# Reordering the first chunks of a test-time-training scan inside a fused decoder block

## The chip, the cores and the metric

One Trainium2 chip, one of its cores. The metric is device time in microseconds (us) for one execution of the whole program.

## The reference, cut to what matters

The program is one decoder block: a test-time-training (TTT) linear attention, a cross-attention and a quantised gated FFN, each followed by a residual sum and a layer norm. The input is 16 sequences of 64 tokens with 256 features. The change touches only the first part, a scan over four chunks of 16 tokens that carries a 16x16 state S for every sequence and head:

```python
def step(S, inp):
    qi, ki, vi, ei = inp
    kh = jnp.einsum('bchd,bhde->bche', ki, S)
    target = vi - ki
    mu = jnp.mean(kh, -1, keepdims=True)
    rstd = jax.lax.rsqrt(jnp.var(kh, -1, keepdims=True) + EPS)
    kh_hat = (kh - mu) * rstd
    g = w * kh_hat + b - target
    gw = g * w
    v_new = (gw - jnp.mean(gw, -1, keepdims=True) - kh_hat * jnp.mean(gw * kh_hat, -1, keepdims=True)) * rstd
    A = jnp.einsum('bchd,bshd->bhcs', qi, ki)
    A = jnp.where(tri, A, 0.0) * jnp.transpose(ei, (0, 2, 1))[:, :, None, :]
    qh = jnp.einsum('bchd,bhde->bche', qi, S) - jnp.einsum('bhcs,bshe->bche', A, v_new)
    o = qi + _ln(qh, w, b)
    S = S - jnp.einsum('bchd,bche->bhde', ki * ei[..., None], v_new)
    return (S, o)
S_fin, o = jax.lax.scan(step, S0, (qc, kc, vc, ec))
```

S starts at zero. Afterwards `o` is gated, normalised per head and multiplied with `Wo`; the cross-attention's keys (`ctx @ Wk`, 16 heads of 128) are independent of the scan.

## The kernel before, in words

Every engine runs a hand-written program in its own order; semaphores tie them together, and there is no planner. The scan's 16 heads lie in two halves of eight, h = 0 and 1, and its four chunks are c = 0 to 3. For a chunk and half the engines do this:

- TensorE (PE): `state_products(c, h)` multiplies the chunk's keys and queries with the state (L538); `scores_ttt(c, h)` makes the scores A (L520 for chunks 0 and 1, L514 for 2 and 3); `own_terms(c, h)` multiplies the corrections with A and the keys, which gives qh and the new state (L548). All are trains of small tiles: 128 recorded matmuls and 128 weight loads a time (64 and 64 for L514).
- VectorE (DVE): `state_read` (L1483 to L1486) takes the products from PSUM; `chain` (L1498 to L1518) turns them into corrections `ub`; `after_own_terms` (L1569, L1573) takes qh and the new state out of PSUM; `a_masked` (L1470) masks the scores and `kb_rows` (L1465) transposes the keys for the own terms; `out_normed`, `out_gated`, `out_c` finish the outputs. Two wide preparations stand ahead of chunk 1: `output_terms` (eight products, L1557, and a transpose, L1560) and `gate_terms` (L1565), which waits for ScalarE's two scalings of the gate (L1097).
- ScalarE (ACT) takes the square roots between `state_read` and `chain` (L1117), squares outputs, spreads keys (`k_blocks`, `k_quads`) and takes the cross-attention keys out of PSUM (L1105, L1107).

Between these steps PE makes the cross-attention keys in 32 units (`key_unit`: two recorded matmuls, L682; after every fourth unit eight short ones, L672, sum the squares of four). `KEY_PLACES` says how many units stand at each place; PE and ACT read the same list. Unit n writes bank 6 or 7 and waits until ACT has emptied unit n - 2.

PE's order ahead of the scan is: a list of jobs (weight transposes and products, the last being `s2` and `w2t`), with `scores_ttt(0, ...)`, `scores_ttt(1, ...)` and `own_terms(0, 0)` put in between; then all jobs must be emptied before the first key unit, and `own_terms(0, 1)` follows that unit.

SyncE (SP) issues the loads in order. Two stand in the scan:

```python
            sp.wait_ge(sem("mg_done"), 2 * 2)
            load_xwq(0)
            load_x()
            roots_to_rows(0)
            sp.wait_ge(sem("og_ready"), 2)
            load_xwq(1)
            load_xwq(2)
            scales_out(0)
            sp.wait_ge(sem("mg_done"), 2 * NCH)
```

`mg_done` counts the own terms (4 is `own_terms(1, 1)`), `og_ready` the gated outputs (2 is `out_gated(1)`). `scales_out(0)` waits for `key_scales(0)` on DVE (L1616), and `load_xwq(3)`, the key scales `rkb` and `ctx` stand behind it.

Of the kernel before, what the change touches and what calls it, by code (L numbers as in the profile page):

```python
# [31 lines left out]
ALU = mybir.AluOpType  # L32
# [6 lines left out]
NCH = T // C  # L39
KT = D // P  # L40
# [12 lines left out]
GW = 2 * C + 32  # L53
NKU = 2 * XH
LT = NT - 1
KEY_PLACES = [(1, 2), (2, 2, 1, 1, 2, 1), (2, 2, 1, 1, 2, 1), (2, 3, 4, 2)]

def decoder_block(nc, x, ctx_in, Wq, Wk, Wv, Wo, Wbeta, ln_w, ln_b, Wg1, Wg2, norm_w,  # L60
                  XWq, XWk, XWv, XWo, gq, gk, w1_in, w2_in, out):
    stack = ExitStack()
    with stack:
# [164 lines left out]
        def bank(n, w=BANK, at=0):  # L228
            return ps[:, n * BANK + at:n * BANK + at + w]
# [6 lines left out]
        def sem(name):  # L236
            if name not in sems:
                sems[name] = stack.enter_context(nc.semaphore(name))
            return sems[name]
# [78 lines left out]
            job("w2t", n, by="act")  # L318
        index_of = {(k, key): n for n, (k, key, _) in enumerate(jobs)}
        job_banks = [n % 8 for n in range(index_of[("s1", (0,))])]  # L320
        job_banks += [(5, 6, 7, 0, 1, 2, 3)[n % 7] for n in range(len(jobs) - 1 - len(job_banks))] + [5]

        def bank_left(n):
            return max(m for m in range(n) if job_banks[m] == job_banks[n])
# [155 lines left out]
        def _(pe):  # L480
# [11 lines left out]
            def done(ins):  # L492
                ins.then_inc(sem("job_done"), 1)
# [7 lines left out]
            def scores_ttt(c, h):  # L501
                if h == 0:
                    if c < 2:
                        pe.wait_ge(sem("kb_ready"), 2 * (c + 1))
                    else:
                        pe.wait_ge(sem("kbq_ready"), 4 * (c - 1))
                    if c >= 1:
                        pe.wait_ge(sem("at_ready"), c)
                if c >= 2:
                    for g in range(B):  # L510
                        for part in (slice(0, 64), slice(64, P)):
                            col = ((c * G + h * B + g) * 2 + 1) * C
                            out = 4 * BANK + (h * B + g) * C
                            last = mm(ps[part, out:out + C], kbq_f[part, h, g * 64:(g + 1) * 64],  # L514
                                      kq[part, col:col + C], start=True, stop=True)
                    last.then_inc(sem("a_done"), 1)
                    return
                for g, j, part in tiles(h):
                    col = ((c * G + g) * 2 + 1) * C
                    last = mm(ps[part, 4 * BANK + g * C:4 * BANK + (g + 1) * C], kb[part, g * 32:(g + 1) * 32],  # L520
                              kq[part, col:col + C], start=True, stop=True)
                last.then_inc(sem("a_done"), 1)
# [19 lines left out]
            def own_terms(c, h):  # L542
                pe.wait_ge(sem("at_ready"), c + 1)
                pe.wait_ge(sem("kbr_ready"), c + 1)
                pe.wait_ge(sem("ub_ready"), 4 * (2 * c + h + 1))
                w = C + 32 if c < NCH - 1 else C
                for g, j, part in tiles(h):
                    last = mm(ps[part, g * GW + C:g * GW + C + w], ub[part, g * 32:(g + 1) * 32],  # L548
                              ak[part, g * (C + 32):g * (C + 32) + w],
                              start=c == 0 and g % (BANK // GW) == 0, stop=True, skip_group_check=True)  # L550
                last.then_inc(sem("mg_done"), 1)
# [81 lines left out]
            for n in range(8):  # L633
# [4 lines left out]
                done(last)  # L638
                if n == 3:
                    scores_ttt(1, 0)  # L640
            scores_ttt(1, 1)
            wait(emptied_by(index_of[("s1", (2,))]))
            pe.wait_ge(sem("diag_ready"), 2)
            bk = open_job("s2", 0)
# [4 lines left out]
            for n in range(2):  # L649
                bk = open_job("w2t", n)  # L650
                o = bank(bk).bitcast(BF16)
                for t in range(3):
                    k = n * 3 + t
                    w = P if k < NK2 - 1 else FFL
                    for r in range(KT):
                        last = nc.tensor.transpose(o[0:w, (t * KT + r) * P:(t * KT + r + 1) * P],
                                                   w2q[:, r * FF + k * P:r * FF + k * P + w], ident_b[:, :])
                done(last)


            def warm(bk, n):
# [33 lines left out]
                    key_unit(next(units))  # L695

            keys(KEY_PLACES[0][0])
            own_terms(0, 1)
            keys(KEY_PLACES[0][1])
            for c in range(1, NCH):  # L700
                places = iter(KEY_PLACES[c])
                state_products(c, 0)
                keys(next(places))
                state_products(c, 1)
                keys(next(places))
                if c < NCH - 1:
                    scores_ttt(c + 1, 0)
                    keys(next(places))
                own_terms(c, 0)
                if c < NCH - 1:  # L710
                    keys(next(places))
                    scores_ttt(c + 1, 1)
                keys(next(places))
                own_terms(c, 1)
                for n in places:
                    keys(n)
# [259 lines left out]
        def _(act):  # L976
# [9 lines left out]
            def emptied(ins):  # L986
                ins.then_inc(sem("prep_act"), 1)

            def job_at(kind, *key):
                n = index_of[(kind, key)]  # L990
                act.wait_ge(sem("job_done"), n + 1)
                return job_banks[n]
# [91 lines left out]
                emptied(A(mvo[:, n * BANK:(n + 1) * BANK], bank(bk), ACT.Copy))  # L1084
            bk = job_at("s2", 0)
            emptied(A(s2[:, :], bank(bk, D), ACT.Copy))
            bk = job_at("w2t", 0)
            emptied(A(w2t[:, 0:3 * D], bank(bk).bitcast(BF16)[:, 0:3 * D], ACT.Copy))
            bk = job_at("w2t", 1)
# [51 lines left out]
            def output_root(n):  # L1141
                root_of(ovs[:, :], osd[:, :], "ovs_ready", n, "osd_ready")
# [8 lines left out]
            def keys(n):  # L1151
                for _ in range(n):
                    key_unit(next(units))

            keys(KEY_PLACES[0][0])
            A(eps_t[:, 2:3], eps_t[:, 1:2], ACT.Sqrt)
            keys(KEY_PLACES[0][1])
            for c in range(1, NCH):
                places = KEY_PLACES[c]
                state_root(c, 0)  # L1160
                if c >= 2:
                    output_root(2 * c - 2)
                output_square(c - 1)
                keys(places[0])
                if c < NCH - 1:
                    k_quads(c + 1)
                keys(places[1])
                output_root(2 * c - 1)
                state_root(c, 1)
                if c < NCH - 1:  # L1170
                    k_blocks(c + 1)
                for n in places[2:-2]:
                    keys(n)
                keys(places[-2])
                if c < NCH - 1:
                    gated_square(c - 1)
                    keys(places[-1])
# [182 lines left out]
        def _(dve):  # L1360
# [172 lines left out]
            def first_chains():  # L1533
# [16 lines left out]
                for h in range(2):  # L1550
                    u_blocks(0, h)

            def output_terms():
                dve.wait_ge(sem("prep_act"), emptied_by(index_of[("gate", (1, 1))])[1])
                for hh in range(KT):
                    for c in range(NCH):
                        V.scalar_tensor_tensor(out=chunk_half(sgR, c, hh), in0=kq_half(1, c, hh), scalar=wb[:, KT + hh:KT + hh + 1],  # L1557
                                               in1=chunk_half(tmp1, c, hh), op0=ALU.add, op1=ALU.mult).then_inc(sem("q_terms"), 1)
                dve.wait_ge(sem("q_terms"), KT * NCH)
                V.transpose(qbR[:, :], sgR[:, :]).then_inc(sem("out_terms"), 1)  # L1560

# [59 lines left out]
            first_chains()  # L1621
            for c in range(1, NCH):
                p_rows(c)
            output_terms()
            after_own_terms(0, 0)
            gate_terms()
            after_own_terms(0, 1)
            for c in range(1, NCH):
                if c == 1:
                    kb_rows(c)  # L1630
                    a_masked(c)
                if c == NCH - 1:
                    key_scales(0)
                state_read(c, 0)
                if c >= 2:
                    kb_rows(c)
                    a_masked(c)
                    output_inverse(2 * c - 2)
                    out_c(c - 2)
                chain(c, 0)  # L1640
                state_read(c, 1)
                output_sums(2 * c - 1)
                output_inverse(2 * c - 1)
                chain(c, 1)
                out_normed()
                after_own_terms(c, 0)
                if c < NCH - 1:
                    out_gated(c - 1)
                else:
                    gated_part(0)  # L1650
                after_own_terms(c, 1)
                if c < NCH - 1:
                    output_sums(2 * c)
# [49 lines left out]
            last_out(0)  # L1703
            last_square(qhR, 2)
            gated_part(1)


            def turn(kind, i, n=0):
# [331 lines left out]
```

## Time and profile before

| | |
|---|---|
| time, median of 3 runs | 373.15 us (372.58 to 373.59) |
| the profiled execution | 372.6 us |
| its span, first to last instruction | 370.9 us |
| mean granted TensorE clock | 0.995 of full speed |
| PE busy | 338.8 us (91%) |
| DVE busy | 265.1 us (71%) |
| ACT busy | 206.9 us (56%) |

The scan runs from about 58 to 141 us of the span; what comes after it is the cross-attention and the FFN. The trace gives for each instruction its engine, its line in the kernel and what released it. "issue" is time in which an engine waited for nothing that the profile shows. The DMA queue called "instruction" carries the engines' own programs.

### The profile page before, as it was taken

The numbers are of one execution on the slowest core, as the hardware profiler recorded it, in microseconds if no ns is written. First come the engines' busy times: TensorE is split into PE (matmuls) and PEld (weight loads), VectorE is DVE, ScalarE is ACT, GpSimd is POOL, SyncE is SP. The second block draws the span as 40 slices with busy tenths as digits, with TensorE's granted clock in tenths as the row PEclk, the third lists the DMA queues.
The fourth block names the chain that finished last, engine by engine and source line by source line (L and its number), as shares of the span: only waits on it lengthen the run. The fifth ranks groups of instructions, "written<-read, shape, count | busy, mean of one in ns | idle before, by whom it ended". The sixth has DMA issues, their size and how long they took to land.

```text
span 370.9 us, 11150 instructions
## 1 busy us (share of the span) xinstructions
PE 338.8 (91%) x4833; PEld 242.4 (65%) x4836; DVE 265.1 (71%) x544; ACT 206.9 (56%) x382; POOL 75.5 (20%) x91
## 2 busy tenths in 40 slices
PE   0999997999899789898999999999999999999974
PEld 0644685565555334787796896987977969866732
DVE  0499989799799999856442855946748549476795
ACT  1245984895665474537246555565565547575351
POOL 3009300000000000000340521623515306300100
PEclk9999999999999899999999999999999999999999
DMA  8998000000502205800050200201101000000000
GB/s 184 281 271 298 4 4 4 4 4 6 171 4 55 75 3 140 151 5 0 4 117 2 58 0 16 60 0 44 30 16 57 2 17 2 0 16 1 16 1 28
DMA packets 17985, 19.94 MB, mean 54 GB/s; under 512 B 3712, under 2 KB 15376, under 8 KB 17680
## 3 DMA queue, kind: packets, MB, share of 16 engines
q1 hardware_dynamic: 17328, 18.69, 19.1%
q10 hardware_dynamic: 608, 0.54, 0.7%
q8 instruction: 38, 0.62, 0.7%
q14 instruction: 11, 0.09, 0.1%
HBM read 18.04 MB, written 1.18 MB: 52 GB/s over the span
## 4 chain that ended last, share of the span: by engine, by line
PE 68%; DVE 22%; ACT 4%; issue 2%; DMA 2%; SPq 0%; POOL 0%; POOLq 0%; DVEq 0%
PE ps L812 14%; PE ps L746 13%; PE ps L567 6%; PE ps L804 5%; PE ps L789 4%; PE ps L831 3%; PE ps L762 2%; PE ps L637 2%; PE ps L682 2%; PE ps L780 2%; DMA xn<-in_x_dram 2%; PE ps L858 1%; PE ps L520 1%; PE ps L548 1%; PE ps L849 1%
## 5 line engine op out<-in xcount | busy, mean ns | idle before, releaser
L746 PEld LDWEIGHTS ps<-x1t,xwq 128*128 128x128 f32 x512 | 59.2, 192 | 6.0 <-issue 4.2
L746 PE MATMUL ps<-x1t,xwq 128*128 128x128 f32 x512 | 62.1, 278 | 0.5 <-ACT x1t L1238 0.5
L812 PE MATMUL ps<-mvo,cxp 128*128 128x256 f32 x224 | 51.8, 383 | 0.5 <-ACT cxp L1249 0.5
L1982 POOL TENSOR_SCALAR rstd<-mv 128x1 f32<-128x1 f32 x20 | 4.4, 218 | 203.2 <-DVE mv L1721 203.2
L812 PEld LDWEIGHTS ps<-mvo,cxp 128*128 128x128 f32 x224 | 41.3, 190 | 6.6 <-ACT cxp L1249 0.8
L1201 ACT ACTIVATE qt<-ps 128x512 f32<-128x512 f32 x32 | 19.1, 596 | 31.7 <-PE ps L746 31.7
L682 PE MATMUL ps<-ctxt,xwk 128*128 128x512 f32 x64 | 34.5, 648 | 1.6 <-ACT w2t L1091 1.2
L1105 ACT ACTIVATE ksq<-ps 128x512 f32<-128x512 f32 x32 | 18.9, 591 | 12.5 <-PE ps L682 8.4
L1107 ACT ACTIVATE kt<-ps,gks 128x512 f32<-128x512 f32 x32 | 22.0, 686 | 0.0
L1208 ACT ACTIVATE qsq<-ps 128x512 f32<-128x512 f32 x32 | 19.0, 593 | 3.2 <-PE ps L762 3.1
L789 PEld LDWEIGHTS ps<-kt,qt 128*64 128x64 f32 x512 | 16.2, 138 | 6.8 <-ACT qt L1201 3.8
L1730 DVE TENSOR_SCALAR x<-rr,mv,rstd 128x256 f32<-128x256 f32 x16 | 6.6, 412 | 18.7 <-POOL rstd L1983 18.5
L804 PE MATMUL ps<-pt,ctx 64*128 64x512 f32 x64 | 18.2, 638 | 0.7 <-ACT pt L1228 0.7
L789 PE MATMUL ps<-kt,qt 128*64 128x64 f32 x512 | 18.4, 225 | 0.0
L682 PEld LDWEIGHTS ps<-ctxt,xwk 128*128 128x128 f32 x64 | 10.8, 197 | 11.4 <-issue 6.5
L1769 DVE TENSOR_TENSOR gs<-ps,s 128x352 f32<-128x352 f32 x16 | 8.3, 523 | 13.4 <-PE ps L831 13.2
L1249 ACT ACTIVATE cxp<-ps 128x512 f32<-128x512 f32 x28 | 15.3, 605 | 4.5 <-PE ps L804 4.5
L1997 POOL TENSOR_TENSOR rq<-rq,mhalf 128x16 f32<-128x16 f32 x6 | 17.4, 2908 | 0.5
L548 PEld LDWEIGHTS ps<-ak,ub 32*32 32x32 f32 x1024 | 11.0, 105 | 9.2 <-issue 9.2
L538 PEld LDWEIGHTS ps<-kqi,st 32*32 32x32 f32 x768 | 10.4, 108 | 9.5 <-issue 9.5
L1793 DVE TENSOR_TENSOR pr<-ps,rkb 128x1024 f32<-128x1024 f32 x8 | 9.8, 1225 | 8.7 <-PE ps L789 8.7
L538 PE MATMUL ps<-kqi,st 32*32 32x64 f32 (+1 forms) x768 | 11.7, 212 | 4.4 <-issue 4.4
(252 smaller groups left out, 692.8 us busy)
## 6 DMA issues: line engine op xcount, KB each, us to landing
rkb<-kscale SPq DMA_DIRECT2D x16, 256.0 KB, 4.3
ctx<-in_ctx_dram SPq DMA_DIRECT2D x4, 512.0 KB, 7.7
xwo<-in_L_xattn_Wo_dram SPq DMA_DIRECT2D x1, 2048.0 KB, 14.2
xwq<-in_L_xattn_Wq_dram SPq DMA_DIRECT2D x4, 512.0 KB, 4.3
w1n<-in_L_ffn_w_gate_up_dram SPq DMA_DIRECT2D x1, 1408.0 KB, 10.1
xwv<-in_L_xattn_Wv_dram SPq DMA_DIRECT2D x1, 1024.0 KB, 11.9
xwk<-in_L_xattn_Wk_dram SPq DMA_DIRECT2D x1, 1024.0 KB, 16.4
xn<-in_x_dram SPq DMA_DIRECT2D x2, 512.0 KB, 6.6
```

What stands on the lines that cost most here:

```text
L538: last = mm(out, st[part, g * 32:(g + 1) * 32], moving, start=g % (BANK // GW) == 0, stop=False, skip_group_check=True)
L567: last = mm(bank(bk), w[:, k * D + hh * P:k * D + (hh + 1) * P], xt[:, k * B * T + half * BANK:k * B * T + (half + 1) * BANK], start=k == ...
L682: mm(bank(6 + n % 2), xwk[:, h * XD:(h + 1) * XD], ctxt[:, half * BANK:(half + 1) * BANK], start=True, stop=True)\
L746: last = mm(bank(n % 2, P, t * P), xwq[qn][:, k * BANK + t * P:k * BANK + (t + 1) * P], x1t[:, (i % 2) * D + k * P:(i % 2) * D + (k + 1) * ...
L789: last = mm(ps[b2 * T:(b2 + 1) * T, 4 * BANK + h * T:4 * BANK + (h + 1) * T], qt[:, h * P + b2 * T:h * P + (b2 + 1) * T], kt[:, (i * XH + ...
L804: turn_done(mm(bank(bk), ctx2[rows, b * CD:(b + 1) * CD], pt[rows, :].rearrange("p (h q) -> p h q", q=P)[:, :, b2 * T:(b2 + 1) * T], start ...
L812: last = mm(bank(turn_banks[turn_of[("y", i, 0)]], D), context_of(i)[:, h * P:(h + 1) * P], mvo[:, h * D:(h + 1) * D], start=h == 0, stop= ...
L1105: A(ksq[n % 4][:, :], bank(6 + n % 2), ACT.Square).then_inc(sem("k_squared"), 1)
L1107: A(o, bank(6 + n % 2).rearrange("p (i t) -> p i t", t=P), ACT.Copy, scale=gks[:, 1:2]).then_inc(sem("key_emptied"), 1)
L1201: A(qt[:, qn * BANK:(qn + 1) * BANK], bank(n % 2), ACT.Copy).then_inc(sem("q_copied"), 1)
L1208: A(qsq[:, (n % 2) * BANK:(n % 2 + 1) * BANK], bank(n % 2), ACT.Square).then_inc(sem("q_squared"), 1)
L1997: GP.tensor_tensor(rq[:, :], rq[:, :], mhalf[:, :], ALU.pow).then_inc(sem("rq_ready"), 1)
```

## The change

On PE, `own_terms(0, 1)` and `state_products(1, 0)` move up behind `own_terms(0, 0)` and the job `w2t`, ahead of all key units; `scores_ttt(1, 1)` moves back behind two key units; and in chunk 1 `own_terms(1, 0)` goes ahead of `scores_ttt(2, 0)`. Chunk 1 holds fewer key units (5 for 9), chunk 2 one more (10) and chunk 3 three more (14). Job `w2t` 0 uses bank 6 instead of 7. On DVE, `output_terms` is split: its eight products are interleaved with `after_own_terms(0, ...)` and its transpose stands behind `kb_rows(1)`; `gate_terms` moves behind `after_own_terms(1, 0)`, `a_masked(1)` behind `chain(1, 0)`, and `key_scales(0)` from the start of chunk 3 to the end of the scan. ACT's program follows.

```diff
 GW = 2 * C + 32
 NKU = 2 * XH
 LT = NT - 1
-KEY_PLACES = [(1, 2), (2, 2, 1, 1, 2, 1), (2, 2, 1, 1, 2, 1), (2, 3, 4, 2)]
+KEY_PLACES = [(2, 1), (1, 3, 1), (2, 2, 2, 1, 2, 1), (3, 4, 5, 2)]
 
 
 
             job("w2t", n, by="act")
         index_of = {(k, key): n for n, (k, key, _) in enumerate(jobs)}
         job_banks = [n % 8 for n in range(index_of[("s1", (0,))])]
-        job_banks += [(5, 6, 7, 0, 1, 2, 3)[n % 7] for n in range(len(jobs) - 1 - len(job_banks))] + [5]
+        job_banks += [(5, 6, 7, 0, 1, 2, 3)[n % 7] for n in range(len(jobs) - 2 - len(job_banks))] + [6, 5]
 
         def bank_left(n):
             return max(m for m in range(n) if job_banks[m] == job_banks[n])
                 done(last)
                 if n == 3:
                     scores_ttt(1, 0)
-            scores_ttt(1, 1)
             wait(emptied_by(index_of[("s1", (2,))]))
             pe.wait_ge(sem("diag_ready"), 2)
             bk = open_job("s2", 0)
                         last = nc.tensor.transpose(o[0:w, (t * KT + r) * P:(t * KT + r + 1) * P],
                                                    w2q[:, r * FF + k * P:r * FF + k * P + w], ident_b[:, :])
                 done(last)
+            wait(emptied_by(index_of[("s2", (0,))]))
+            own_terms(0, 1)
+            state_products(1, 0)
 
 
             def warm(bk, n):
                     key_unit(next(units))
 
             keys(KEY_PLACES[0][0])
-            own_terms(0, 1)
+            scores_ttt(1, 1)
             keys(KEY_PLACES[0][1])
-            for c in range(1, NCH):
+            state_products(1, 1)
+            keys(KEY_PLACES[1][0])
+            own_terms(1, 0)
+            scores_ttt(2, 0)
+            keys(KEY_PLACES[1][1])
+            own_terms(1, 1)
+            scores_ttt(2, 1)
+            keys(KEY_PLACES[1][2])
+            for c in range(2, NCH):
                 places = iter(KEY_PLACES[c])
                 state_products(c, 0)
                 keys(next(places))
                 emptied(A(mvo[:, n * BANK:(n + 1) * BANK], bank(bk), ACT.Copy))
             bk = job_at("s2", 0)
             emptied(A(s2[:, :], bank(bk, D), ACT.Copy))
+            A(eps_t[:, 2:3], eps_t[:, 1:2], ACT.Sqrt)
             bk = job_at("w2t", 0)
             emptied(A(w2t[:, 0:3 * D], bank(bk).bitcast(BF16)[:, 0:3 * D], ACT.Copy))
             bk = job_at("w2t", 1)
                 for _ in range(n):
                     key_unit(next(units))
 
-            keys(KEY_PLACES[0][0])
-            A(eps_t[:, 2:3], eps_t[:, 1:2], ACT.Sqrt)
-            keys(KEY_PLACES[0][1])
-            for c in range(1, NCH):
+            state_root(1, 0)
+            output_square(0)
+            keys(sum(KEY_PLACES[0]))
+            k_quads(2)
+            output_root(1)
+            state_root(1, 1)
+            k_blocks(2)
+            keys(KEY_PLACES[1][0] + KEY_PLACES[1][1])
+            gated_square(0)
+            keys(KEY_PLACES[1][2])
+            for c in range(2, NCH):
                 places = KEY_PLACES[c]
                 state_root(c, 0)
-                if c >= 2:
-                    output_root(2 * c - 2)
+                output_root(2 * c - 2)
                 output_square(c - 1)
                 keys(places[0])
                 if c < NCH - 1:
                 for h in range(2):
                     u_blocks(0, h)
 
+            def query_terms(hh):
+                dve.wait_ge(sem("prep_act"), emptied_by(index_of[("gate", (1, 1))])[1])
+                for c in range(NCH):
+                    V.scalar_tensor_tensor(out=chunk_half(sgR, c, hh), in0=kq_half(1, c, hh), scalar=wb[:, KT + hh:KT + hh + 1],
+                                           in1=chunk_half(tmp1, c, hh), op0=ALU.add, op1=ALU.mult).then_inc(sem("q_terms"), 1)
+
             def output_terms():
-                dve.wait_ge(sem("prep_act"), emptied_by(index_of[("gate", (1, 1))])[1])
-                for hh in range(KT):
-                    for c in range(NCH):
-                        V.scalar_tensor_tensor(out=chunk_half(sgR, c, hh), in0=kq_half(1, c, hh), scalar=wb[:, KT + hh:KT + hh + 1],
-                                               in1=chunk_half(tmp1, c, hh), op0=ALU.add, op1=ALU.mult).then_inc(sem("q_terms"), 1)
                 dve.wait_ge(sem("q_terms"), KT * NCH)
                 V.transpose(qbR[:, :], sgR[:, :]).then_inc(sem("out_terms"), 1)
 
             first_chains()
             for c in range(1, NCH):
                 p_rows(c)
+            query_terms(0)
+            after_own_terms(0, 0)
+            query_terms(1)
+            after_own_terms(0, 1)
+            kb_rows(1)
             output_terms()
-            after_own_terms(0, 0)
-            gate_terms()
-            after_own_terms(0, 1)
             for c in range(1, NCH):
-                if c == 1:
-                    kb_rows(c)
-                    a_masked(c)
-                if c == NCH - 1:
-                    key_scales(0)
                 state_read(c, 0)
                 if c >= 2:
                     kb_rows(c)
                     output_inverse(2 * c - 2)
                     out_c(c - 2)
                 chain(c, 0)
+                if c == 1:
+                    a_masked(c)
                 state_read(c, 1)
                 output_sums(2 * c - 1)
                 output_inverse(2 * c - 1)
                 chain(c, 1)
                 out_normed()
                 after_own_terms(c, 0)
+                if c == 1:
+                    gate_terms()
                 if c < NCH - 1:
                     out_gated(c - 1)
                 else:
             last_out(0)
             last_square(qhR, 2)
             gated_part(1)
+            key_scales(0)
 
 
             def turn(kind, i, n=0):
```

## Rows read from the trace of the kernel before

**Rows 1.** The page: the chain that ended last by engine, and the instruction queue.
```profile
q8 instruction: 38, 0.62, 0.7%
...
PE 68%; DVE 22%; ACT 4%; issue 2%; DMA 2%; SPq 0%; POOL 0%; POOLq 0%; DVEq 0%
```

**Rows 2.** Timeline of DVE, 57 to 120 us: start, us, line, operation, count.
```profile
57.98 3.21 DVE L1557 SCALAR_TENSOR_TENSOR sgR<-kqi,wb,tmp 128x256 f32<-128x256 f32 x8
61.23 2.31 DVE L1560 STREAM_TRANSPOSE qbR<-sgR 128x2048 f32<-128x2048 f32 x1
...
66.99 2.31 DVE L1565 STREAM_TRANSPOSE sgR<-tmp 128x2048 f32<-128x2048 f32 x1 [2.37 <-ACT tmp L1097]
...
70.31 1.20 DVE L1465 STREAM_TRANSPOSE ak<-kb 128x1024 f32<-128x1024 f32 x1
...
72.01 0.43 DVE L1483 STREAM_TRANSPOSE khR<-ps 128x256 f32<-128x256 f32 x1
...
73.73 0.25 DVE L1498 RECIPROCAL rs<-sdc 128x16 f32<-128x16 f32 x1 [0.38 <-ACT sdc L1117]
...
82.35 0.25 DVE L1498 RECIPROCAL rs<-sdc 128x16 f32<-128x16 f32 x1
...
88.23 0.69 DVE L1589 TENSOR_TENSOR oR<-qhR,ors 128x512 f32<-128x512 f32 x1
...
91.72 0.45 DVE L1569 STREAM_TRANSPOSE qhR<-ps 128x256 f32<-128x256 f32 x1 [0.27 <-PE ps L548]
...
92.84 0.65 DVE L1577 TENSOR_REDUCE ovs<-osq 128x32 f32<-128x512 f32 x1
95.30 0.45 DVE L1483 STREAM_TRANSPOSE khR<-ps 128x256 f32<-128x256 f32 x1 [1.81 <-PE ps L538]
...
117.75 0.45 DVE L1569 STREAM_TRANSPOSE qhR<-ps 128x256 f32<-128x256 f32 x1
...
119.44 0.54 DVE L1616 RECIPROCAL kinv<-kinv 128x64 f32<-128x64 f32 x1
119.90 0.39 DVE L1483 STREAM_TRANSPOSE khR<-ps 128x256 f32<-128x256 f32 x1
```

**Rows 3.** Timeline of PE, 57 to 130 us: start, us, line, operation, count, wait.
```profile
61.72 1.13 PE L548 MATMUL ps<-ak,ub 32*32 32x48 f32 x87 [1.52 <-issue]
...
85.14 1.07 PE L672 MATMUL ps<-ksq,onehot 128*32 128x512 f32 x8
86.13 2.04 PE L514 MATMUL ps<-kqi,kbq 64*64 64x16 f32 x64
88.10 1.98 PE L682 MATMUL ps<-ctxt,xwk 128*128 128x512 f32 x4
90.02 1.56 PE L548 MATMUL ps<-ak,ub 32*32 32x48 f32 x128
...
94.82 0.42 PE L538 MATMUL ps<-kqi,st 32*32 32x64 f32 x15 [0.45 <-issue]
...
124.83 1.07 PE L538 MATMUL ps<-kqi,st 32*32 32x32 f32 x64 [2.60 <-issue]
125.84 3.17 PE L682 MATMUL ps<-ctxt,xwk 128*128 128x512 f32 x4
```

**Rows 4.** Busy time and instruction counts of each engine in stretches; then PEclk, DMA.
```profile
61.70:94.50 32.80, 31.00 (x1020) 19.56 (x1021) 27.30 (x58) 23.94 (x42) 0.00 (x0) 1.00 0.06 19
...
122.30:128.30 6.00, 3.46 (x67) 2.12 (x68) 5.69 (x14) 2.44 (x5) 0.00 (x0) 0.72 0.07 19
```

**Rows 5.** DMA queues in three windows: 92.0 to 92.5, 92.5 to 98.8, 98.8 to 101.0 us.
```profile
q8 instruction: 1, 0.02, 14.3%
...
q1 hardware_dynamic: 1250, 1.50, 77.6%
...
q8 instruction: 1, 0.02, 2.9%
```

**Rows 6.** Timeline of SP's queue, 80 to 125 us: issue start, us, transfer.
```profile
91.64 0.38 SPq L388 DMA_DIRECT2D xwq<-in_L_xattn_Wq_dram  x1
```

## The prediction

> **What bounds the kernel now.** I read the chain that ended last first. Over the whole run it is mostly PE [rows 1], but in the scan it changes hands: PE up to 95.30 us, where DVE waits for PE's product [rows 2], and DVE from there to the scan's end. So I then read DVE's timeline [rows 2], where the reader should look at start times, since one start less the one before it is what a step costs in its queue, and at the bracket, the idle time ahead of it. DVE is nearly always at work; its two large gaps ahead of chunk 2 are 2.37 us ahead of `gate_terms` and 1.81 us ahead of `state_read(2, 0)` at 95.30, where it waits for PE. From 95.30 on its order is the same in both kernels, so a delay or gain of that read goes to the end, unless PE falls behind.
>
> PE's timeline [rows 3] shows why it may. Its small-tile trains stop four times between 57 and 130 us with the remark "issue": 1.52, 0.45, 1.37 and 2.60 us (three of the four stand there). The instruction counts between the first two stops are 1020 + 1021 = 2041 [rows 4], eight times 256 but for seven, and the view does not count separate waits; the queue "instruction" moved 0.62 MB in 38 packets, 16 KB each [rows 1]. So I take PE to get its program in blocks of 256, and a stop to be a block that came late. The block of the 0.45 us stop was fetched just after 92.0 us and could be used at 94.82; the next one was not fetched until after 98.8 [rows 5], though its turn came at 94.82 when PE went on. In between, 1.50 MB of SP's first load (issued at 91.64 [rows 6]) passed. The 2.60 us stop is the same thing after SP's second load, which `out_gated(1)` releases at 117.75 [rows 2]. Fetches asked for during a load waited for about its tail; I saw three of three do so.
>
> **The change part by part: DVE.** I lay its new order end to end. The products of half 0, 57.98 to 59.6 (four of eight in 3.21 us). `own_terms(0, 0)` now starts without the `scores_ttt(1, 1)` that stood ahead of it, near 58.4, and takes 1.5 (as 90.02 to 91.51, rounded from [rows 3]): 59.9. Taking it out costs 1.1 (91.72 to 92.84): 61.1. Products of half 1: 62.7. `own_terms(0, 1)` follows `w2t` (0.9) but crosses a block's edge so soon after the last one that I give it a stop of 1.3, near the 1.52 [rows 3] that `own_terms(0, 0)` loses: it ends at 63.6 and DVE waits 0.9. Out: 64.8; `kb_rows` 1.1 and the wide transpose 2.25: 68.2. `state_read(1, 0)` starts here, not at 72.01, and PE's product for it is done by 67.4 (63.6, 1.9 of work and one more stop, up to 1.9). Read and root 1.7 (72.01 to 73.73); from one chain's start to the next 8.6 (73.73 to 82.35) plus `a_masked` 0.6; chain 5.9; out_normed, out of PSUM and gating 3.2 (88.23 to 91.72 less 0.27); `gate_terms` 2.3, whose scalings are long done; out again 1.1, sums 0.6. That ends at 92.2, 3.1 before 95.30 [rows 2]. ACT's earlier square-root table (its load lies beside PE's transposes) costs nothing here: `w2t` is not needed until the key units near 67.4. If that cover were gone, it would delay key units only.
>
> **PE in the same stretch** keeps up: `own_terms(1, 1)` ends at 87.1 (four units and the stops put PE 0.5 behind DVE's corrections at 85.0), then scores 2.0, a unit 1.0 and `state_products(2, 0)` 1.9: 92.0. So far the change is worth 3 us.
>
> **The load.** `own_terms(1, 1)` at 87.1 releases SP's first load, 4.5 us earlier than before, since the wait is on that step. Its traffic runs to about 94.4 (as 91.64 to 98.9 [rows 5, 6]). In the kernel before, a block ends 226 instructions into `state_products(2, 0)`'s 256 (all but 15 of 128 matmuls with their loads [rows 3]). The change takes four key units and four sums, 32 instructions, out of what precedes it and adds one wait, so the edge comes 257 after its start: in the key unit right behind it. That block can be asked for when the one before is begun, 256 earlier, at 89 to 90. Before, that moment lay ahead of the load's first byte (fetched at 92.0, load from 92.5); now it lies inside it. Fetched at 94.4 and usable 2.3 later (before it was 2.3 to 2.8, from 92.0 to 92.5 until 94.82), it lets PE go on at 96.7, after a stop of 4.6 us. A 2.60 us stop was followed by the lower granted clock (1.2 GHz level; mean 0.72 over 122.3 to 128.3 [rows 4]), under which four key matmuls took 3.17, not 1.98 [rows 3]; I charge up to 1.6 for it here, that 1.2 and some 0.4 for the rest of the stretch.
>
> What is late next: from 96.7 PE has 20.4 us of work to the end of `own_terms(2, 1)` (half a unit 0.5, eight units 8.0, three sets of sums 3.0, two scores 4.0, a product 1.9, two own terms 3.0 [rows 3]): 117.1, or 118.7 with the clock. DVE wants it 22.4 after its read (95.30 to 117.75), at 114.7. ACT empties these late units ahead of `output_root(3)`, for which DVE's chain waits about 1 more. So DVE waits 2 to 3 us, and its `out_gated(1)` releases SP's second load near 116, just ahead of the fetch that `state_products(3, 0)` needs (asked for near 118). That fetch comes at the load's tail, 120.5 (4.7 after its release: before, 117.75, and usable at 124.83, so fetched near 122.5), and is usable at 122.8; before, the same load hit the next block, which DVE did not need yet. `state_products(3, 0)` ends at 123.4 to 124, so `state_read(3, 0)` is at 123.5 to 124.1, not 119.90: 3.6 to 4.2 late.
>
> **The rest.** `key_scales(0)` leaves a place where PE is now the later one and adds 0.46 (119.44 to 119.90) where DVE sets the end. Chunk 3's three extra units (1.25 us each with their sums) fill PE's idle time but leave `own_terms(3, 0)` and `(3, 1)` just at DVE's heels: 0.4. SP's queue behind `scales_out(0)`, with `load_xwq(3)`, `rkb` and `ctx`, starts only after the scan's tail; the first of them is wanted by PE's fourth query quarter, after the first norms, so I charge nothing and leave up to 1 us to the range; a miss would show as PE waiting at L746. Sum: 3.9 + 0.5 + 0.4 = 4.8 us over the profiled 372.6, 377.4. The median shown stands 0.55 above that execution; I forecast 377.6.
>
> **Weighed against the skill.** The trace shows four stops at block edges [rows 3]. The Trainium skill, "Runtime: NRT & Kernel Launch", section "Instruction fetch mechanics", says that the sequencer fetches 256-instruction blocks by itself and that the cost is mostly hidden. The block's size agrees with [rows 1]; the hiding does not hold in these trains, and by it the time would be that of rival 2. For the fetch's place in a load, "DMA: Bandwidth & Descriptors" of the Trainium skill, section "Queues, rings and completion order", has an engine take turns between rings packet by packet; [rows 5] shows a wait to the tail, and by the page the time would be that of rival 1.
>
> **Rivals.** *1. The loads do not hold blocks back.* Then PE stops only 1.1 after `state_products(2, 0)` (asked for at 90, 0.8 to start, 2.3 to use) and ends `own_terms(2, 1)` about 114 to 115, even with DVE's 114.7; chunk 3 loses 1 to another edge and 0.9 as above. DVE's 3.1 is used up: 0 ± 0.7, 373.2. For it: one block went by just ahead of the load. Against: three fetches that waited. *2. No block is ever late, or edges fall harmlessly.* DVE reads at 91.3, `state_products(3, 0)` ends at 116.7, 3.2 early, less 0.5, 0.4 and about 0.6 of new waits on key units: 1.7 faster, 371.4. This one ends on the other side; it decides if the stop behind `state_products(2, 0)` stays under about 1 us. *3. Only one load hits*: 2.3 to 4.0 slower, 376. *4. The edge lies a few instructions earlier*, inside `state_products(2, 0)`: DVE itself waits until 97, and the second load follows: 9 to 10 slower, 383.
>
> **How the numbers follow.** Changes under 0.3% (1.1 us) are about what a measurement of this kernel cannot tell from none. Forecast 0.46 (its own range 375.5 to 379.8, from a fetch at two thirds of the load without the clock's price to the full one with it); rival 1 0.18, rival 2 0.20, rival 3 0.11, rival 4 0.05. Slower 0.46 + 0.11 + 0.05 = 0.62, same 0.18, faster 0.20. The range 371.9 to 380 leaves out rival 4 and most of rival 2.
>
> **What would show it.** Right: `state_read(2, 0)` near 92 instead of 95.30; then a stop of 4 to 5 us marked "issue" at a key unit (L682) behind L538 near 92, a lower granted clock after it, DVE waiting ahead of L1569 or L1483 near 115 to 124, SP's first load near 87. Wrong: no such stop, or a stop that DVE never waits for; then the 3 us stay. If `state_read(2, 0)` itself is not early, my sum over DVE's queue failed.

## The result, and the profile after

The changed kernel takes 378.89 us (median of 4, 378.18 to 379.12) against 373.37 for the kernel before in the same comparison: slower, ratio 1.0134, 95% interval 1.0092 to 1.0176. The profiled execution took 379.12 us with a span of 377.4 and a mean granted clock of 0.982 (before: 372.6, 370.9, 0.995). The forecast was 377.6. Ratios here and below leave out runs more than 1.5% above the fastest of their kernel; medians are over all runs.

The whole difference is in the scan: the first `rw` behind it (DVE's first residual sum) starts at 154.10 instead of 147.45, 6.65 us later, and the spans of the two profiled executions differ by 6.5. Where it went is plainest in the view of waits, for DVE from 57 to 148 us: operation, what it waited for, us in total, times, the longest. First the kernel before, then the kernel after.

```profile
DVE sgR L1565 <- ACT tmp L1097: 2.4, 1, 2.4
DVE khR L1483 <- PE ps L538: 1.8, 1, 1.8
DVE ors L1581 <- ACT osd L1117: 1.2, 3, 0.4
DVE rs L1498 <- ACT sdc L1117: 0.4, 1, 0.4
DVE qhR L1569 <- PE ps L548: 0.3, 1, 0.3
```

```profile
DVE khR L1500 <- PE ps L538: 5.1, 3, 3.1
DVE qhR L1587 <- PE ps L548: 3.8, 4, 2.9
DVE ors L1599 <- ACT osd L1128: 3.4, 3, 1.7
DVE rs L1515 <- ACT sdc L1128: 0.4, 1, 0.4
```

The wait ahead of `gate_terms` (`sgR`) is gone, as meant. In its place DVE waits 3.3 us more for state products, 3.5 more for own terms and 2.2 more for roots: 12.7 us, not 6.1. These waits are 6.6 of the 6.65 us. PE's timeline after shows why it is late (start, us, line, tiles, count, idle before); these lines answer to [rows 3].

```profile
65.06 1.64 PE L538 MATMUL ps<-kqi,st 32*32 32x64 f32 x101 [1.91 <-issue]
66.63 1.98 PE L684 MATMUL ps<-ctxt,xwk 128*128 128x512 f32 x4
...
77.46 0.69 PE L514 MATMUL ps<-kqi,kbq 64*64 64x16 f32 x17
79.46 2.18 PE L514 MATMUL ps<-kqi,kbq 64*64 64x16 f32 x47 [1.30 <-issue]
81.57 2.07 PE L684 MATMUL ps<-ctxt,xwk 128*128 128x512 f32 x2
83.58 1.94 PE L674 MATMUL ps<-ksq,onehot 128*32 128x512 f32 x8
85.44 2.74 PE L684 MATMUL ps<-ctxt,xwk 128*128 128x512 f32 x4
88.11 1.56 PE L548 MATMUL ps<-ak,ub 32*32 32x48 f32 x128
...
92.63 1.99 PE L538 MATMUL ps<-kqi,st 32*32 32x64 f32 x128
94.55 0.70 PE L684 MATMUL ps<-ctxt,xwk 128*128 128x512 f32 x1
98.18 1.22 PE L684 MATMUL ps<-ctxt,xwk 128*128 128x512 f32 x1 [2.93 <-issue]
99.33 1.94 PE L674 MATMUL ps<-ksq,onehot 128*32 128x512 f32 x8
...
119.95 1.56 PE L548 MATMUL ps<-ak,ub 32*32 32x48 f32 x128
...
124.43 0.59 PE L538 MATMUL ps<-kqi,st 32*32 32x32 f32 x45 [1.03 <-issue]
```

Two stops matter: 1.30 us inside `scores_ttt(2, 0)` and 2.93 in the key unit behind `state_products(2, 0)`. Behind each, eight key sums take 1.94 us where they took 1.07 [rows 3]. The windows of these stretches give the reason. Each line has the stretch, its length, the busy time of PE, PE's weight loads, DVE, ACT and POOL, then the granted clock and the DMA share. The clock is 0.57 and 0.50 of full speed, the 1.2 GHz level for most or all of the stretch.

```profile
79.45:87.40 7.95, 7.94 (x60) 3.73 (x60) 7.63 (x18) 1.98 (x5) 0.00 (x0) 0.57 0.01 2
98.20:103.20 5.00, 5.00 (x11) 0.97 (x11) 4.72 (x11) 1.18 (x2) 0.00 (x0) 0.50 0.02 3
```

The second stop has SP's load in it, as [rows 5] had it for another block. The DMA queues after, in 89.6 to 95.7 us (the load alone, no packet of the instruction queue) and in 95.7 to 98.2 (the load's last 0.09 MB and the block):

```profile
q1 hardware_dynamic: 1224, 1.48, 77.0%
...
q8 instruction: 1, 0.02, 2.8%
```

DVE's timeline after, to be held against [rows 2]:

```profile
90.94 0.64 DVE L1595 TENSOR_REDUCE ovs<-osq 128x32 f32<-128x512 f32 x1
94.69 0.45 DVE L1500 STREAM_TRANSPOSE khR<-ps 128x256 f32<-128x256 f32 x1 [3.11 <-PE ps L538]
...
121.65 0.45 DVE L1587 STREAM_TRANSPOSE qhR<-ps 128x256 f32<-128x256 f32 x1 [2.85 <-PE ps L548]
...
125.07 0.45 DVE L1500 STREAM_TRANSPOSE khR<-ps 128x256 f32<-128x256 f32 x1 [1.65 <-PE ps L538]
...
138.95 0.35 DVE L1599 RECIPROCAL ors<-osd 128x32 f32<-128x32 f32 x1 [1.36 <-ACT osd L1128]
...
153.63 0.55 DVE L1634 RECIPROCAL kinv<-kinv 128x64 f32<-128x64 f32 x1
154.10 0.36 DVE L1864 TENSOR_TENSOR rw<-ps,xn 128x256 f32<-128x256 f32 x1
```

### The profile page after: what moved, and what is told of

Same layout as the page of the kernel before. It is cut to its first block, busy times and chain, and to the rows that moved or that the text cites. A ratio compares the mean times of both kernels' runs of the same rounds, so it can differ in the third digit from the quotient of the medians.

```text
span 377.4 us, 11154 instructions
## 1 busy us (share of the span) xinstructions
PE 343.3 (91%) x4836; PEld 243.4 (65%) x4836; DVE 265.3 (70%) x544; ACT 207.3 (55%) x382; POOL 75.6 (20%) x91
## 4 chain that ended last, share of the span: by engine, by line
PE 75%; DVE 15%; ACT 4%; issue 3%; DMA 2%; SPq 0%; POOL 0%; POOLq 0%; DVEq 0%; ACTq 0%
PE ps L822 14%; PE ps L756 13%; PE ps L684 6%; PE ps L567 5%; PE ps L814 5%; PE ps L799 4%; PE ps L548 3%; PE ps L841 3%; PE ps L514 2%; PE ps L772 2%; PE ps L674 2%; PE ps L637 2%; PE ps L538 2%; PE ps L790 2%; DMA xn<-in_x_dram 2%
## 5 line engine op out<-in xcount | busy, mean ns | idle before, releaser
L684 PE MATMUL ps<-ctxt,xwk 128*128 128x512 f32 x64 | 37.2, 685 | 6.0 <-ACT kt L1118 3.1
```

Of the source, the lines that this page charges most:

```text
L684: mm(bank(6 + n % 2), xwk[:, h * XD:(h + 1) * XD], ctxt[:, half * BANK:(half + 1) * BANK], start=True, stop=True)\
```

## The experiments

Theory 1: program blocks that come late, SP's load on top of them and the lower clock behind them make PE late. (An edge is the place in PE's program where one block of 256 instructions ends and the next begins.) Theory 2: the key units were handed out badly, with ACT emptying them in order. Theory 3: DVE's moved steps cost by themselves. The list of waits speaks against theory 3 already, since nearly all of the loss is time in which DVE waits for PE or ACT.

**The load, 12 us later.** In the kernel after and, as a control, in the kernel before:

```diff
 sp.wait_ge(sem("mg_done"), 2 * 2)
+sp.wait_ge(sem("kh_done"), 4)
 load_xwq(0)
 load_x()
```

> The kernel after, with SP's first load (the query weights and x, 1.5 MB) released by the second state product of chunk 2 instead of by own_terms(1, 1): some 12 us later, and behind the program block that stopped PE for 2.93 us in key unit 8. Theory 1 (program blocks that come late, one of them held back by this load, make PE late, and the lower clock after a stop adds to it): the stop at key unit 8 falls from 2.93 to 0.5 to 1.1 us, the key units behind it run at full clock, DVE's wait of 2.85 ahead of the copy for own_terms(2, 1) goes to under 1, state_read(3, 0) is at 121.5 to 122.5 instead of 125.07, and the total is 2.5 to 3.5 us less than the kernel after, 375.4 to 376.4. Theory 2 (the key units were handed out badly, and ACT, which empties them in order, is late with the roots): the order on PE and ACT is untouched, so less than 1 us. Theory 3 (the steps moved on DVE cost by themselves): less than 0.5 us.

> Control: the same later release of SP's first load in the kernel before. There the block held back by that load comes due while DVE has PE's results in hand, so theory 1 expects a smaller stop on PE in chunk 2 and 0 to 0.5 us off the total (372.9 to 373.4). Were the load costly in some other way (traffic of its own beside DVE and ACT), the total would fall by 1 us or more here too. Theories 2 and 3: no change.

After: 375.88 us, ratio to before 1.0085 (1.0055 to 1.0114). PE's timeline: the stop in the key unit is 0.91, the sums behind it take 1.07.

```profile
96.20 0.70 PE L685 MATMUL ps<-ctxt,xwk 128*128 128x512 f32 x1 [0.91 <-issue]
96.82 1.07 PE L675 MATMUL ps<-ksq,onehot 128*32 128x512 f32 x8
```

`state_read(3, 0)` starts at 121.30 (0.2 sooner than forecast), and DVE's wait ahead of the copy for `own_terms(2, 1)` is 0.64, as theory 1 said. The same edit in the kernel before gives 374.21, ratio 1.003 (0.9998 to 1.0061), above the 372.9 to 373.4 that I expected: in its trace the stops of 0.45 and 1.37 are gone (one of 0.21 is left), and still there is no gain. So the load costs through the block it holds back, where DVE waits for that block's work, and not by its traffic.

**The edges alone.** Only the places where PE's program is cut are moved, by matmuls at the start where PE idles until 8.2 us: 64 of them, half a block, and 128, a whole block, as the control.

```diff
 pe.wait_ge(sem("consts"), 2)
+for _ in range(64):
+    mm(bank(7)[0:32, 0:32], ident_b[0:32, 0:32], ident_b[0:32, 0:32], start=True, stop=True)
```

> The kernel after, with 64 matmuls of 32 columns (128 instructions) put ahead of PE's first work, where PE otherwise idles until 8.2 us: nothing in the scan's order changes, only the places at which PE's program is cut into blocks of 256 move by half a block. Theory 1: the stops marked issue appear at other instructions, and the total moves by 1 us or more; I expect 2 us less than the kernel after, 377, with half the chance that an edge lands inside a state product and it is 1 us more. Theories 2 and 3: within 0.5 us of the kernel after.

> Control for the run with half a block: 128 such matmuls (256 instructions), one whole block, so that the edges fall on the same instructions of the scan again while PE does twice the extra work at the start. Theory 1: the stops at the same instructions as in the kernel after and the total within 0.5 us of it. If the extra work at the start matters by itself (warmer clock, other fetches at the start), this run moves as the one with half a block does.

A whole block: 378.93 us (1.0154, 1.0109 to 1.0198), the kernel after again, with its stop in the same key unit (3.38). Half a block: 384.27 (1.0287, 1.0232 to 1.0341), 5.3 us slower than that, though every order is the same; its fastest run, 380.75, lies above the slowest with a whole block, 380.02. Theories 2 and 3 have no place for it. I had the sign wrong. PE's timeline of the half block shows the stops elsewhere:

```profile
82.23 1.06 PE L676 MATMUL ps<-ksq,onehot 128*32 128x512 f32 x8
...
85.66 1.56 PE L548 MATMUL ps<-ak,ub 32*32 32x48 f32 x128
...
89.03 1.93 PE L514 MATMUL ps<-kqi,kbq 64*64 64x16 f32 x61 [1.60 <-issue]
...
95.78 1.09 PE L538 MATMUL ps<-kqi,st 32*32 32x64 f32 x63 [1.08 <-issue]
```

Without a stop in `scores_ttt(2, 0)` the sums take 1.06 and `own_terms(1, 1)` starts at 85.66 instead of 88.11. But the next block, due inside `state_products(2, 0)` itself, was fetched only near the load's tail (load issued at 87.28, fetch at 93.39, use at 95.78), and DVE waits 4.53 for that product. This is rival 4's mechanism.

**The edge of the change, in the kernel before.** 112 such matmuls put the edge behind `state_products(2, 0)`, as after; then the same with the later load.

> The kernel before, with 112 matmuls of 32 columns (224 instructions) ahead of PE's first work, in time in which PE idles. All orders are those of before; the program edge that fell 226 instructions after the start of state_products(2, 0) now falls 258 after it, in the key unit behind, which is where the change puts it (257). Theory 1 (an edge there asks for its block inside SP's first load and stops PE in the key unit): a stop of 3 to 5 us marked issue at the key unit behind state_products(2, 0), where before had 0.45 inside the product, DVE waiting for PE late in chunk 2, and a total 3 to 5 us above before, 376.5 to 378 on the scale of 373.4. Theory 2 (the handing out of the key units) and theory 3 (the steps moved on DVE): neither is touched, so within 0.5 us of before.

> The kernel before with its edges moved by 224 instructions, as in the run before_edge_moved, whose times fell into two groups (370.8 to 376.3 and 377.6 to 379.8), and with the first load released 12 us later. Theory 1 (the two groups are a race of one block's fetch against the first byte of the load): the upper group is gone, all times between 371 and 375, median 372 to 373.5. If something else makes the two groups: they are there again.

376.94 us over 12 runs, but in two groups: 370.83 to 376.26 and 377.62 to 379.80. The ratio of 1.0024 (0.9986 to 1.0063) is of the lower group. The profiled run, 374.17, is of that group: its fetch, at 92.91, went through in the middle of the load (issued at 90.15, traffic until 97.9), and the stop was 1.25. So a load does not hold back every fetch. With the later load the median is 374.67 (0.9986, 0.9948 to 1.0024), again in two groups (371.29 to 373.20 and 376.14 to 379.99), so the race that I expected between load and fetch is not what makes the two groups. They go with the granted clock: over both kernels it is 0.991 to 0.993 in ten of the twelve lower runs and 0.974 to 0.986 in eleven of the twelve upper ones. The two traces, 374.17 and (with the later load) 376.91, show one place of it: in both PE waits 3.03 us for DVE in chunk 3, and behind that wait the clock is at the lower level for about twice as long in the second (a mean of 0.81 and of 0.62; fields as above).

```profile
132.00:141.00 9.00, 7.87 (x159) 3.31 (x163) 8.16 (x24) 4.86 (x10) 0.00 (x0) 0.81 0.01 3
133.00:142.00 9.00, 8.63 (x143) 3.88 (x144) 8.16 (x25) 3.24 (x7) 0.00 (x0) 0.62 0.01 3
```

Why the same wait is followed by more or less of it stays open. The edge there alone did not make the kernel slower in every run; this prediction of theory 1 held for half of them and not for the cause given.

**DVE's part alone.** The kernel before with `gate_terms` moved as in the change:

```diff
 after_own_terms(0, 0)
-gate_terms()
 after_own_terms(0, 1)
...
     after_own_terms(c, 0)
+    if c == 1:
+        gate_terms()
```

> One part of the change alone: the kernel before, with DVE's gate_terms moved from chunk 0 behind the first own terms of chunk 1, as the change has it; PE, ACT and SP keep the orders of before, so every block edge stays. If DVE sets chunk 1's time, its wait of 2.37 goes and the total falls by 1 to 2 us. If PE does (the trace has state_products(1, 0) at 69.40 only because own_terms(0, 1) and key units stand ahead of it): state_read(1, 0) moves by 0.5 at most, the wait ahead of state_read(2, 0) shrinks from 1.81 toward 0, and the total stays within 0.5 us of before.

373.04 us, ratio 1.0000 (0.9975 to 1.0024). The wait of 2.37 is replaced by one of 3.06 ahead of the copy for `own_terms(0, 1)`, and `state_read(1, 0)` is at 71.81 instead of 72.01. The move is worth nothing unless PE is sooner, and costs nothing either. Of DVE's moved steps only this one was tested alone; for the others theory 3 falls by the list of waits.

**Is PE in hand behind chunk 1?** First, ACT takes chunk 3's roots two key units sooner:

```diff
-keys(places[1])
+late = 2 if c == NCH - 1 else 0
+keys(places[1] - late)
 output_root(2 * c - 1)
 state_root(c, 1)
+keys(late)
```

> The kernel after, with ACT taking the two roots of chunk 3 (output_root(5), state_root(3, 1)) behind the fifth of chunk 3's key units instead of the seventh; PE, DVE and SP untouched. Theory 2: DVE's wait of 1.36 us ahead of output_inverse(5) falls to about 0.4 and the total by 0.5 to 1.0 us (377.9 to 378.4). Theory 1 alone: PE sets the end there, ACT's place does not matter, within 0.3 us of the kernel after.

DVE's wait fell from 1.36 to 0.39 as theory 2 said, and the total rose to 382.44 (1.0269, 1.0238 to 1.0301). PE's key sums now wait for ACT, and the own terms behind them come late. In the traces this makes the scan 2.0 us longer; another 1.2 us lies behind the scan (below). PE's timeline, then DVE's:

```profile
138.80 1.05 PE L674 MATMUL ps<-ksq,onehot 128*32 128x512 f32 x2 [1.24 <-ACT ksq L1116]
```

```profile
148.84 0.45 DVE L1589 STREAM_TRANSPOSE qhR<-ps 128x256 f32<-128x256 f32 x1 [2.80 <-PE ps L548]
```

Second, with the later load, what DVE waits for in chunk 2 is put sooner on PE:

```diff
 own_terms(1, 1)
+state_products(2, 0)
 scores_ttt(2, 1)
...
 for c in range(2, NCH):
...
-    state_products(c, 0)
+    if c > 2:
+        state_products(c, 0)
```

> The kernel with the later first load (375.9), and state_products(2, 0) ahead of scores_ttt(2, 1) on PE, so that DVE gets what it waits 3.0 us for some 2 us sooner. It asks whether what DVE loses there is lost for good or whether PE is the late engine through all of chunk 2 anyway. As the prediction had it (DVE sets the end from state_read(2, 0) on): state_read(2, 0) at 92.6 to 93.2 instead of 94.73, and the total 1.5 to 2 us less, 374. If PE's own work sets the end of chunk 2 (its work is only put in another order): state_read(2, 0) as early, but DVE waits as much more ahead of the copy for own_terms(2, 1) or of state_read(3, 0), and the total within 0.5 us of 375.9.

`state_read(2, 0)` came at 92.64, 2.1 sooner, and the total was 378.73 (1.0153, 1.0114 to 1.0193), 2.9 more than 375.88. Both forecasts miss: PE stopped 1.43 inside the product and went on at a clock of 0.58 (92.5 to 100.6), and ACT, in order, held `output_root(2)` behind a key unit that was now late. One run of the six had a granted clock of 0.991 and took 374.73, near the first forecast; the other five had 0.973 to 0.986 and took 377.76 to 379.42. So the miss is one of the clock at least in part. DVE's timeline:

```profile
92.64 0.45 DVE L1503 STREAM_TRANSPOSE khR<-ps 128x256 f32<-128x256 f32 x1 [1.64 <-PE ps L539]
...
98.91 0.35 DVE L1602 RECIPROCAL ors<-osd 128x32 f32<-128x32 f32 x1 [2.92 <-ACT osd L1131]
```

**The first stop.** The later load, and 80 matmuls at the start, which put the edge of `scores_ttt(2, 0)` behind it:

> The kernel with the later first load (375.9), and 80 matmuls of 32 columns (160 instructions) ahead of PE's first work, which moves the program edge that lay inside scores_ttt(2, 0) (a stop of 1.30 us in the kernel after, 1.57 with the later load) behind it, among key units; orders unchanged. Theory 1 (that stop and the lower clock behind it cost PE 2.5 us, and PE is the late engine from there to the end): no stop in scores_ttt(2, 0), the eight key sums behind it in about 1.06 us instead of 1.94, own_terms(1, 1) at 85.5 to 86 instead of 88.15, and the total 1.5 to 2.5 us less than 375.9, 373.4 to 374.4. If the clock's fall there is not from the stop, the sums take 1.9 again. If DVE's slack ahead of gate_terms hides it, the total stays within 0.5 us of 375.9.

The step itself went as expected: at 81.41 the eight sums take 1.06, the clock is 1.00 from 79.4 to 87.4, and `own_terms(1, 1)` starts at 85.59. The total did not: 383.71 (1.0283, 1.0253 to 1.0313), since all later edges moved too. PE's timeline:

```profile
85.59 1.43 PE L549 MATMUL ps<-ak,ub 32*32 32x48 f32 x115 [0.69 <-DVE ub L1538]
89.25 0.36 PE L549 MATMUL ps<-ak,ub 32*32 32x48 f32 x13 [2.23 <-issue]
...
131.53 0.31 PE L539 MATMUL ps<-kqi,st 32*32 32x32 f32 x12 [3.32 <-issue]
131.78 5.66 PE L687 MATMUL ps<-ctxt,xwk 128*128 128x512 f32 x8
```

The 3.32 us is SP's second load: issued at 124.99, the block's fetch starting at 129.14, use at 131.53. Eight key matmuls behind it take 5.66 (four take 1.98 [rows 3]), and DVE waits 5.96 for a root behind them.

**PE's work itself.** With the later load, one key unit is moved from chunk 2 to the end of chunk 3, behind the last own terms; then also the one ahead of `state_products(2, 0)` is put behind it:

```diff
-KEY_PLACES = [(2, 1), (1, 3, 1), (2, 2, 2, 1, 2, 1), (3, 4, 5, 2)]
+KEY_PLACES = [(2, 1), (1, 3, 1), (2, 2, 1, 1, 2, 1), (3, 4, 5, 3)]   # after_unit_to_tail
+KEY_PLACES = [(2, 1), (1, 3, 0), (3, 2, 1, 1, 2, 1), (3, 4, 5, 3)]   # after_two_units_later
```

> The kernel with the later first load (375.9), and one key unit of PE and ACT moved from chunk 2 to the end of chunk 3, behind own_terms(3, 1), where PE otherwise fills time with idle matmuls. If PE with ACT behind it sets the end through chunks 2 and 3: 0.5 to 1.2 us less, 374.7 to 375.4, with DVE's waits ahead of the copy for own_terms(2, 1) and of state_read(3, 0) (0.64 and 1.75) smaller together by about 1. If DVE sets it: within 0.3 us. If the extra unit on ACT delays the last root: 0.5 us more.

> The kernel of after_unit_to_tail (374.08, the later first load and one key unit of chunk 2 at the end of chunk 3), with also the key unit ahead of state_products(2, 0) moved behind it. In after_unit_to_tail DVE still waits 2.78 us ahead of state_read(2, 0), while PE has 0.98 us in hand at own_terms(2, 1). If PE's key units ahead of state_products(2, 0) are what DVE waits for: state_read(2, 0) about 1 us sooner, PE's 0.98 in hand used up, and the total 0.5 to 1 us less, 373.1 to 373.6, level with the kernel before; it would be the best order of the change's parts that these runs point to. If PE, already late, only puts it off to chunk 2: state_read(2, 0) sooner, DVE waiting as much more at own_terms(2, 1) or state_read(3, 0), and the total within 0.3 us of 374.1.

One unit: 374.08 us, ratio 1.0034 (1.0008 to 1.0060), 1.8 less than with the later load alone and more than the unit's own 1.25 us. Part of that may be theory 2's, but the run does not separate it from the edges: the one in `state_products(3, 0)` is gone too (its stop was 1.14). In its trace PE waits for DVE at `own_terms(2, 1)` (0.98), and DVE's total wait for roots is 1.2, as before the change. The two units: 375.63 (1.0054, 1.0026 to 1.0082), not less; that it is more is not clear, since the two ratios' intervals overlap. The edge now lies three matmuls into `state_products(2, 0)`, and the product runs at the lower clock (PE's timeline; DVE waits 4.27 for it):

```profile
93.41 3.38 PE L539 MATMUL ps<-kqi,st 32*32 32x64 f32 x125 [0.56 <-issue]
```

No version with the whole change beat the kernel before; the best stays 0.34% above it.

**Behind the scan.** In five of these profiled executions (half a block, ACT's root sooner, the state product first, no stop in the scores, the moved edge with the later load) PE's clock falls once more just behind the scan. Over 154 to 166 us its mean is 0.86 in the run without the stop in the scores, for example, and 1.00 in the kernel after. From the first `rw` to the end these five take 224.4 to 224.5 us, all others 223.3 to 223.4. So 1.1 us of each of these five spans is not the scan's.

## Why the prediction was right, point by point

The sign and the size came out (377.6 against 378.89), the size in part by luck. In the profiled executions the scan lost 6.65 us where the sum had 4.8. PE's lateness ahead of the first load was missing from the sum, that load's stop was too large in it, and the second load, which the sum let hit, did not. By its own figures (372.6, 4.8, and 0.55 for the median) the sum gives 377.95.

**DVE's queue**: right. DVE was through its sums at 91.58 (92.2 forecast), 3.7 us ahead of the 95.30 at which the kernel before read the product.

**"PE in the same stretch keeps up: `own_terms(1, 1)` ends at 87.1"**: wrong, and this is the step that failed. It ended at 89.67, the product at 94.62 (92.0 forecast). The stop in `scores_ttt(2, 0)` was not in the sum, nor the clock behind it. The rows at the lower clock cost 0.95 + 0.87 + 0.76 (2.07, 1.94 and 2.74 against 1.12, 1.07 and 1.98), the stop 1.30; without them, in two runs, the own terms start at 85.59 and 85.66, 2.5 us sooner and where the sum had them. So of DVE's 3.7 us, 0.6 reached `state_read(2, 0)` (94.69 instead of 95.30).

**The load and the stop behind `state_products(2, 0)`**: the mechanism and place were right, the size was not: 2.93, not 4.6. PE came to the edge at 95.25, 3.1 later than in the sum (92.1), but the block came only 1.5 later (98.18, not 96.7). The load was issued 2.6 late, at 89.73, and the fetch started at its tail, at 95.76, 6.0 us behind the issue where the sum had 7.3. With its clock the stop is worth 3.0 us by the medians of one comparison (378.93 with a whole block, which is the kernel after again, and 375.88 with the later load); nine of the ten runs with the later load (374.75 to 377.11) lie below all four of the kernel after. The Trainium skill says of the cost of crossing a block's boundary that it is "mostly hidden" ("Runtime: NRT & Kernel Launch", section "Instruction fetch mechanics"). By that the time would not change when the edges alone move; here it changed by 5.3 us.

**PE late at `own_terms(2, 1)`**: right, DVE waits 2.85 (2 to 3 forecast).

**"`out_gated(1)` releases SP's second load near 116"**: wrong. I left out that `roots_to_rows(0)` stands ahead of it in SP's queue and that its roots come later when the key units do. SP's timeline after:

```profile
124.38 1.33 SPq L427 DMA_DIRECT2D kroot<-krow  x4
...
127.45 0.94 SPq L388 DMA_DIRECT2D xwq<-in_L_xattn_Wq_dram  x2
```

The load comes behind `state_products(3, 0)`; its stop of 1.03 stays at 1.14 with the later first load and is that of two edges close together. The mechanism does exist: with other edges the second load cost 3.32 (above). `state_read(3, 0)` was 5.17 late all the same, not 3.9: PE's lateness with its two clock drops, and a wait of 1.69 for a root of ACT's in chunk 2.

**The rest**: `key_scales` 0.47 from its start to the next (0.46 forecast). Chunk 3 lost 1.0, not 0.4: 1.36 for a root that ACT reaches only behind its seventh key unit, 0.39 before.

**Against the rivals.** Rival 1 (loads hold nothing back) falls for the kernel after with the later load, though one fetch, at 92.91 in the run with the moved edge, did go through inside a load. What the loads did in the kernel after is rival 3's case (chance 0.11), only the first one hit; its 376 is too low by PE's lateness ahead of it. As to rival 2 (no block late), none of these runs had the blocks harmless. What is shown is that the edges' places alone decide over 5 us. In the trace of the kernel after PE does not wait 0.2 us or more for DVE once between 57 and 145 us: DVE waits for PE, not the other way round. That without any late block the change would gain is not shown.

## What to carry to other kernels

A step taken off one engine's queue is only worth what the next engine in the chain can give: list that engine's work in the same stretch, stops included, before counting the gain. Work that fills gaps (here key units) is not free to move: put behind the point where it was hidden, it brings its emptying engine's order and the transfers that wait for it along. Where an engine runs thousands of small instructions, try the same order with its program shifted by half a block before judging an order by a few microseconds: such a shift alone moved this kernel by 5.3 us, as much as the change itself. And a few microseconds can be the clock's: here one order fell into two groups some 5 us apart that went with the granted clock.

## What was not expected of the hardware

A stop as short as 1.30 us was followed by some 7 us near the lower clock (mean 0.57), and one of 0.56 by a product of 3.38 instead of 1.99. Not every stop is: behind the one of 1.91 us ahead of 65.06 in the kernel after, four key matmuls took 1.98, full speed. A mean clock of 0.982 over 377.4 us is 13.6 us at the lower level, if all the rest ran at full speed, against 3.7 before.

From the start of a fetch to the first instruction of its block took 2.2 to 2.7 us in six stops of four runs (2.18 at the stop in the scores and 2.42 at the one in the key unit of the kernel after). In the run without the stop in the scores, one fetch began at 86.60 although, counted from that run's stops, the block ahead of it had been begun near 81.4; between 81 and 87 us the DMA queues moved nothing but this one packet. What delayed it stays open.
